# An LSTM recommender on one Trainium2 core: the head's bias sum moved to GpSimd, the sum over the days of the week to VectorE, and the opening of VectorE reordered

## What is computed

```python
rp = concat([region_tbl[region_idx], poi_tbl[poi_idx]])
nv = concat([rp @ W_rp + b_rp, coords @ W_co + b_co])
conv = elu(conv1d(nv, conv_w) + conv_b)                   # 8 steps of 32
emb = tanh(concat([car_tbl[car_idx], week_tbl[week_idx], time_tbl[time_idx]]))
x = concat([conv, emb for every step])
h = lstm_layer(x, Wih0, Whh0, bih0, bhh0)
h = lstm_layer(h, Wih1, Whh1, bih1, bhh1)
return ((h[:, -1] @ W1 + b1) @ W2 + b2) @ W3 + b3
```

## Time and profile before

| what | value |
|---|---|
| median of three runs | 1087.03 us |
| the profiled execution: time, and its span | 1081.45 us, 1079.6 us |
| TensorE busy | 1061.9 us, 98% |
| VectorE busy | 741.5 us, 69% |
| ScalarE busy | 516.4 us, 48% |
| GpSimd busy | 328.7 us, 30% |
| mean granted TensorE clock | 0.996 of full speed |
| chain that ended last | TensorE 88%, VectorE 6% |

### The profile page before, as it was taken

The page is one execution under the profiler, slowest core; times in us unless marked ns, Lnnn a source line. Parts: engine busy times, 40 slices in busy tenths (PEclk is TensorE's granted clock), DMA queues, the critical chain, the costliest instruction groups (busy, mean ns, idle before and its releaser), DMA issues.

```text
span 1079.6 us, 14388 instructions
## 1 busy us (share of the span) xinstructions
PE 1061.9 (98%) x4905; PEld 508.5 (47%) x4905; DVE 741.5 (69%) x1155; ACT 516.4 (48%) x757; POOL 328.7 (30%) x353
## 2 busy tenths in 40 slices
PE   8899999999999999999999999999999999999998
PEld 7544444444445444444445444444444444444445
DVE  6688866765767766666867865567676775666554
ACT  3665344454555444434554544345554544444433
POOL 7660255625410065533440045552450000000000
PEclk9899999999999999999999999999999999999999
DMA  9410100000101100000101010000010110000001
GB/s 265 84 18 1 31 2 3 2 1 2 31 1 40 31 4 3 2 2 2 16 18 40 1 34 2 2 2 1 2 31 1 40 30 0 2 0 1 1 1 39
DMA packets 32082, 21.26 MB, mean 20 GB/s; under 512 B 19629, under 2 KB 25865, under 8 KB 32019
## 3 DMA queue, kind: packets, MB, share of 16 engines
q1 hardware_dynamic: 21223, 19.25, 6.2%
q0 software_dynamic: 9984, 1.12, 2.6%
q10 hardware_dynamic: 812, 0.07, 0.1%
HBM read 9.92 MB, written 4.19 MB: 13 GB/s over the span
## 4 chain that ended last, share of the span: by engine, by line
PE 88%; DVE 6%; issue 2%; ACT 2%; SPq 1%; DMA 1%; DVEq 0%; ACTq 0%
PE acc L1509 49%; PE acc L1500 27%; PE acc L1494 4%; PE aux L1731 2%; SPq L495 1%; PE aux L1422 1%; PE acc L1562 1%; PE acc L1571 1%; ACT gates L835 1%; DVE h_full L1188 1%; DVE gates L1141 1%; DVE h_part L1189 1%; ACT tanh_c L840 1%; PE aux L1461 1%; DMA w_nat<-in_L_rec_Wih 1%
## 5 line engine op out<-in xcount | busy, mean ns | idle before, releaser
L1509 PE MATMUL acc<-h_part,wh 128*128 128x512 f16 (+1 forms) x2640 | 644.2, 380 | 0.0
L1509 PEld LDWEIGHTS acc<-h_part,wh 128*128 128x128 f16 x2640 | 240.3, 98 | 314.2 <-issue 54.6
L1500 PE MATMUL acc<-h_part,wh 128*128 128x512 f16 (+1 forms) x1440 | 346.8, 379 | 0.0
L835 ACT ACTIVATE gates<-acc,gate_bias,unscale 128x512 f32<-128x512 f32 x246 | 189.8, 778 | 303.2 <-PE acc L1509 283.6
L835 ACT ACTIVATE gates<-gates,gate_bias,unscale 128x512 f32<-128x512 f32 x242 | 188.6, 810 | 141.6 <-DVE gates L1141 141.0
L1500 PEld LDWEIGHTS acc<-h_part,wh 128*128 128x128 f16 x1440 | 139.9, 98 | 171.4 <-issue 4.8
L652 POOL DMA_INDIRECT feat<-in_L_rec_region_tbl,region_idx x160 | 162.1, 1013 | 165.0 <-PE acc L1509 132.8
L1141 DVE TENSOR_TENSOR gates<-acc,emb_gates 128x512 f32<-128x512 f32 x242 | 160.2, 685 | 42.5 <-PE acc L1509 33.4
L652 POOL DMA_INDIRECT feat<-in_L_rec_poi_tbl,poi_idx x120 | 121.4, 1012 | 109.6 <-PE acc L1509 97.3
L1494 PE MATMUL acc<-x_in,wx 96*128 96x512 f32 (+1 forms) x242 | 134.8, 563 | 3.7 <-DVE gates L1141 2.5
L1188 DVE TENSOR_TENSOR h_full<-gates,tanh_c 128x512 f32<-128x512 f32 x120 | 82.7, 689 | 75.3 <-ACT tanh_c L840 75.3
(11 more groups left out here) (182 smaller groups left out, 418.6 us busy)
## 6 DMA issues: line engine op xcount, KB each, us to landing
out<-y SPq DMA_DIRECT2D x16, 256.0 KB, 2.1
x_in<-conv_hi SPq DMA_DIRECT2D x56, 64.0 KB, 2.0
feat<-in_L_rec_region_tbl,region_idx POOLq DMA_INDIRECT x160, 2.3
w<-in_L_rec_W SPq DMA_DIRECT2D x4, 512.0 KB, 6.4
w_nat<-in_L_rec_Whh SPq DMA_DIRECT2D x2, 1024.0 KB, 8.6
w<-in_L_rec_W SPq DMA_DIRECT2D x1, 2048.0 KB, 11.9
feat<-in_L_rec_poi_tbl,poi_idx POOLq DMA_INDIRECT x120, 2.3
x_in<-conv_lo SPq DMA_DIRECT2D x28, 64.0 KB, 2.0
```

The lines of the kernel that those rows point to most:

```text
L835: nc.scalar.activation(gates[layer][:, j, g, :], source, ACT.Tanh if g == GATE_G else ACT.Sigmoid, bias=gate_bias[:, layer, m:m + 1], scal ...
L1500: mm = nc.tensor.matmul(bank, wh[:, 1, a, c, rows], h_part[0][:, s.write_slot, b, c, :], start=(c == 0 and a == b == HI), stop=(s.first an ...
L1509: mm = nc.tensor.matmul(bank, wh[:, own_w, a, c, rows], h_part[layer][:, s.read_slot, b, c, :], start=False, stop=(c == HK - 1 and a == LO))
```

## The change

Three things are moved.

1. VectorE's opening: the third row maximum goes from in front of `put_band` to behind `put_conv_bias`, and `row_scales(1)` goes behind `put_wx_lo`.
2. The sum over the days of the week: GpSimd keeps the product, and its copy and six adds become one `tensor_reduce` on VectorE, behind `add_biases`.
3. The head's constant: VectorE's eight instructions go. GpSimd, behind its last gather of the first batch, multiplies the eight slices of `w3` in place by their column of `b12` and adds them up in seven adds. TensorE's product with the ones stands in front of `cell(fifth)` and no longer behind it, and so does VectorE's add of b3.

```diff
--- before.py
+++ after.py
@@ -381,6 +381,7 @@
         w12_acc, w12_put = sem("w12_acc"), sem("w12_put")
         head_acc, head_hi_put, head_low_put = sem("head_acc"), sem("head_hi_put"), sem("head_low_put")
         b12_ready = sem("b12_ready")
+        head_sum_scaled = sem("head_sum_scaled")
         one_ready, head_sum_step, head_bias_acc, head_bias_put = (sem("one_ready"), sem("head_sum_step"),
                                                                   sem("head_bias_acc"), sem("head_bias_put"))
         coords_first_put = sem("coords_first_put")
@@ -618,12 +619,6 @@
                 nc.gpsimd.tensor_tensor(week_part[:, :, :, :], week_hot[:, :, :].unsqueeze(2).to_broadcast(rows),
                                         week_tbl[:, :, :].rearrange("p w d -> p d w").unsqueeze(1).to_broadcast(rows),
                                         ALU.mult).then_inc(week_step, 1)
-                pool.wait_ge(week_step, 2)
-                nc.gpsimd.tensor_copy(week_rows[:, :, :], week_part[:, :, :, 0]).then_inc(week_step, 1)
-                for day in range(1, WEEK):
-                    pool.wait_ge(week_step, day + 2)
-                    nc.gpsimd.tensor_tensor(week_rows[:, :, :], week_rows[:, :, :], week_part[:, :, :, day], ALU.add
-                                            ).then_inc(week_step if day + 1 < WEEK else week_put, 1)
 
             def poi_parts():
 
@@ -637,6 +632,21 @@
                         nc.gpsimd.tensor_tensor(poi_rest[:, k, :], rest[:, :] if k == 0 else poi_rest[:, k - 1, :],
                                                 poi_part[:, k, :], ALU.subtract).then_inc(poi_part_step, 1)
                         pool.wait_ge(poi_part_step, k + 1)
+
+            def sum_head_bias():
+
+                pool.wait_ge(head_acc, 2)
+                pool.wait_ge(b12_ready, 1)
+                for k in range(K2):
+                    nc.gpsimd.tensor_scalar(w3[:, k, :], w3[:, k, :], b12[:, k:k + 1], None, ALU.mult
+                                            ).then_inc(head_sum_scaled, 1)
+                pool.wait_ge(head_sum_scaled, 2)
+                nc.gpsimd.tensor_tensor(head_sum[:, :], w3[:, 0, :], w3[:, 1, :], ALU.add).then_inc(head_sum_step, 1)
+                for k in range(2, K2):
+                    pool.wait_ge(head_sum_scaled, k + 1)
+                    pool.wait_ge(head_sum_step, k - 1)
+                    nc.gpsimd.tensor_tensor(head_sum[:, :], head_sum[:, :], w3[:, k, :], ALU.add
+                                            ).then_inc(head_sum_step, 1)
 
             for n in range(NB):
                 tiles = None
@@ -703,6 +713,7 @@
                         landed = rows_in[0 if t < WIN else 1]
                         gather_steps(t, t + 1, False, landed)
                         pool.wait_ge(landed, (t - (PAIR_WIN if t < WIN else WIN) + 1) * GR * DMA)
+                    sum_head_bias()
                 else:
 
                     for c in range(CH):
@@ -967,6 +978,11 @@
                                         .to_broadcast([P, NB * GR, WEEK]),
                                         week_number[:, :].unsqueeze(1).to_broadcast([P, NB * GR, WEEK]),
                                         ALU.is_equal).then_inc(week_step, 1)
+            def sum_week():
+                dve.wait_ge(week_step, 2)
+                nc.vector.tensor_reduce(week_rows[:, :, :], week_part[:, :, :, :], AX.X, ALU.add
+                                        ).then_inc(week_put, 1)
+
             def row_maxima(i):
                 dve.wait_ge(w_in[i], DMA)
                 nc.vector.tensor_reduce(row_max[:, i, :], w_nat[i][:, :, :], AX.X, ALU.max,
@@ -1039,17 +1055,6 @@
                 dve.wait_ge(w12_put, K2)
                 dve.wait_ge(b2_put, 1)
                 nc.vector.tensor_tensor(b12[:, :], w12_t[:, :, H], b2_col[:, :], ALU.add).then_inc(b12_ready, 1)
-
-            def sum_head_bias():
-
-                dve.wait_ge(w3_in, DMA)
-                dve.wait_ge(b12_ready, 1)
-                nc.vector.tensor_scalar(head_sum[:, :], w3[:, 0, :], b12[:, 0:1], None, ALU.mult
-                                        ).then_inc(head_sum_step, 1)
-                for k in range(1, K2):
-                    dve.wait_ge(head_sum_step, k)
-                    nc.vector.scalar_tensor_tensor(head_sum[:, :], w3[:, k, :], b12[:, k:k + 1], head_sum[:, :],
-                                                   ALU.mult, ALU.add).then_inc(head_sum_step, 1)
 
             def put_head_lo(a):
                 dve.wait_ge(head_hi_put, a + 1)
@@ -1267,13 +1272,14 @@
             poi_one_hot(3, POI_PIECES)
             row_maxima(1)
             put_poi()
-            row_maxima(2)
             put_band()
             put_conv_bias()
+            row_maxima(2)
+            put_wx_lo()
             row_scales(1)
-            put_wx_lo()
             put_wh_lo(0)
             add_biases()
+            sum_week()
             elu(0, slice(0, HALF), (0, slice(0, HALF)), ())
             put_wh_lo(1)
             split_emb(0)
@@ -1297,14 +1303,13 @@
             indices(1, "region", REG, later, (later_idx_in, 2 * DMA))
             cell(third)
             cell(fourth)
-            sum_head_bias()
             dve.wait_ge(idx_ready, 2)
             indices(2, "poi", POI, later, (later_idx_in, 2 * DMA))
             elu(chunk_of(0, 1), slice(0, NCOL), (1, slice(0, NCOL)), [])
-            cell(fifth)
             dve.wait_ge(head_bias_acc, 1)
             dve.wait_ge(b3_in, DMA)
             nc.vector.tensor_tensor(b_head[:, :], aux[:, 0, :], b3_row[:, :], ALU.add).then_inc(head_bias_put, 1)
+            cell(fifth)
 
             for stage in stages(dve, NB, STEPS):
                 kind = stage[0]
@@ -1426,7 +1431,7 @@
 
             def sum_head_bias():
                 pe.wait_ge(one_ready, 1)
-                pe.wait_ge(head_sum_step, K2)
+                pe.wait_ge(head_sum_step, K2 - 1)
                 nc.tensor.matmul(aux[:, 0, :], one_col[:, 0:1].to_broadcast([P, P]), head_sum[:, :], start=True,
                                  stop=True).then_inc(head_bias_acc, 1)
 
```

## The result

| | before | after |
|---|---|---|
| median of six runs each, alternated | 1090.37 us (1086.82 to 1091.85) | 1099.26 us (1098.05 to 1099.39) |
| profiled execution, its span | 1081.45, 1079.6 us | 1098.76, 1096.9 us |
| GpSimd busy | 328.7 us | 350.2 us |

The change is **slower: ratio 1.0088, interval 1.0071 to 1.0104**, 8.9 us. The forecast was 0.9 us on a median of 1087.03, in a range that ended at 1093.2.

A forecast was written before the change was run, and what follows sets the result against it. TensorE, 98% busy, was taken to bound the kernel: the opening gains 4.0 us, VectorE's lag 2.1, the wait on GpSimd costs 6.9, so 0.9 us slower on 1087.03, 1087.9 us; range 1082.4 to 1093.2.

The forecast's parts named there:

- the gathers 2.6 us earlier: Opening: with the week's copy and adds off GpSimd, the next gather starts at 23.8 us, not 26.47, 2.65 us earlier.
- a wait in front of the ones' product: Before the fifth cell: TensorE waits 4 to 7 us for GpSimd's sum; 6.9 us was booked.
- two-input products on VectorE: Beside GpSimd's sum: VectorE's products with both inputs in SBUF take 1 to 2 us in place of 0.68.
- The adds, with their turns: GpSimd's head sum: seven adds at 1.50 us plus 0.06 between; turns with VectorE add 4.9 us over the whole sum.
- It costs nothing while that gap stays: Week's reduction on VectorE: its 0.4 us fits into VectorE's 0.90 us wait ahead of `elu`, and its readers come later.
- All later gathers are paced by GpSimd itself and by landings: First batch's later gathers on GpSimd: they also move 2.65 us earlier, so the engine comes free at 81.4 us.
- rival 4: Opening: rows land no earlier or GpSimd's pace isn't its own; GpSimd starts at 84.0 us, time 1090.5 us; 6%.
- The products: GpSimd's head sum: eight products of 128x512 with a column, 0.65 us each plus 0.06 between.
- rival 3: GpSimd's head sum: a product with a column costs an add's 1.56 us, not 0.71; time 1094.7 us; 12%.
- The sum: GpSimd's head sum before the fifth cell: 16.6 us alone plus 4.9 of turns with VectorE, from 81.4 to 102.9 us.
- VectorE's lag: Behind the fifth cell: 6.0 us of head bias work leaves VectorE, so TensorE's waits for it vanish, 2.1 us gained.
- The opening: First part of the kernel: earlier gathers and less idle time at the lower clock put TensorE 4.0 us earlier.

The follow-up runs named there:

- e9: Changed kernel with the week's sum left on GpSimd, VectorE's reduction gone: 1094.46 us, ratio 1.0054 to the kernel before; the changed kernel beside it took 1100.84 us.
- e2: Changed kernel with the ones' product and VectorE's add of b3 back behind the fifth cell, on the first chip: 1079.42 us, ratio 0.9988 to the kernel before.
- e3: Changed kernel with the head sum wholly back on VectorE and the ones' product behind the fifth cell, first chip: 1079.34 us, ratio 0.9988 to the kernel before.
- e6: Third chip: kernel before 1091.67 us, changed kernel 1099.88, changed with ones' product behind the fifth cell 1092.78, changed with head sum back on VectorE 1094.06.
- e4: Kernel before with only the week's reduction moved to VectorE, behind the biases, on the first chip: 1078.36 us, ratio 0.9981 to the kernel before.
- e8: Fourth chip: changed kernel 1099.62 us; kernel before with only the week's reduction on VectorE 1095.60; changed kernel with that reduction placed earlier 1109.29.
- e7: Second chip: week's reduction earlier on VectorE, in the changed kernel 1105.02 us, in the kernel before 1099.39; kernel before with 23 added GpSimd passes 1115.29.
- e1: Kernel before, unchanged, run again on the first chip: 1080.47 us, ratio 0.9997 to its other runs there.

## Why the prediction was wrong

Right were: the gathers 2.6 us earlier; a wait in front of the ones' product of 4 to 7 us (5.1 to 6.7 in all six profiles of the change); no gap behind it; two-input products on VectorE at 1 to 1.6 us beside the sum, evictions from PSUM unchanged at 1.87 for three. The adds, with their turns, were booked at 1.56 each plus a share of 4.9 us; they measured 1.28 once and 1.61 six times, turns taken in.

**The step that failed** is "It costs nothing while that gap stays ... Its readers, GpSimd's copy and SP's first stores of x, come later", and with it "All later gathers are paced by GpSimd itself and by landings". That was true of the one trace and is true on the first chip (36.30 against 38.60). But the reduction ties GpSimd's later gathers to VectorE's queue, while in the kernel before GpSimd waited for nothing of VectorE's there. On chips with slow issue VectorE is late: with the reduction in its program it stands 15.6 to 17.5 us at the points of interest, for nothing that the profile names. GpSimd now stands for 13.7 us, ends at 118.4 and not at 102.9, and TensorE, which comes at 113.4 where it came at 100.07, still waits for it. This was rival 4's condition ("GpSimd's pace is not its own"), priced at a start of 84.0 and given 6%; the start was 92.87. With the reduction off VectorE, 6.4 us of the 10.1 are gone (e9). How much of them needs VectorE's stand is not shown. An estimate from e9's rows: without the stand VectorE is past the biases at 46.0, a reduction there would let GpSimd go on at some 46.7 and not 51.5, the sum would end near 114, and TensorE would wait 1 to 2 us. So the tie alone would cost little; the tie and the stand together cost most of the 6.4.

**Mis-sized terms.** The products were taken at 0.65 us, from copies; they measured 1.70 in e2 and 1.81 after, and 1.48 at the least. That is rival 3's mechanism, at 12%. The sum took 24.6 us (e2) and 25.3 to 25.9 (the six profiles of the change), not 21.5. On chips with slow issue that alone costs next to nothing: in e9 the sum ends at 111.9 and TensorE comes at 112.34. VectorE's lag, booked at 2.1 us, was worth 0.1 (e2 against e3) or 1.3 (e6). The opening, booked at 4.0, gave 1.3 with the new order (e3) and 2.3 without it (e4), in part because the first rows were turned 0.9 us earlier and not 2.65. And the wait cost 1.5 us more than its length, for the clock behind it.

**What was under my eyes.** The profiled execution stood 5.6 us under the median of its three runs. I added the difference to the end as if it lay outside the places of the change. In e6 it lies in them (the ones' product at 132.42 and not 120.79): every slack read from that trace was that of an opening without the stall.

**What stays open.** The changed kernel never ran on the first chip. An estimate there, from e2: TensorE comes to the place at 98.35 (e2's convolution piece at 97.33 and its 1.02), the sum ends at 104.9, so 6.5 us of wait and 1.5 of clock on 1079.4, about 1087: slower than 1080.65 by some 0.6%, mostly for the dear products. Open too is the rest of 3.8 us in e9, and the 4.0 us that the reduction alone costs in e8. The opening's stall differs by program: the kernel with the reduction early takes 4.8 us (e7) and 9.7 us (e8) longer than the changed kernel, which differs in one line's place. That alone could hold both. Why the stall is there at all, and why VectorE's part of it comes with the reduction in its program, was not found. The Trainium skill (Runtime: NRT & Kernel Launch, "Instruction fetch mechanics") says that instructions stream in by blocks through a queue of the engine's own, at a cost that is mostly hidden; no run here shows whether that is what stalls.

No version beat the kernel before on both kinds of chip: the reduction alone gains 2.3 us on one (e4) and loses 4.0 on the other (e8).

## What to carry to other kernels

Before a small step moves to another engine, read what stands ahead of it in that engine's queue and whom that waits for: with 0.49 us of work on VectorE an engine that had run free was tied to one that was late, and without it the kernel was 6.4 us faster. A slack read from one trace is the slack of that execution; where the profiled time and the median differ by more than runs do, look for the difference before using any gap. And a relief counts only on the engine that the end waits for: 6 us taken off VectorE gave 0.1 to 1.3.

## What was not expected of the hardware

- Chips differ in the opening: with the same program and the same transfers TensorE gets 123 (e1) or 82 (e6) products through from 20 to 46 us. It is worth 11 us.
- The stall is not one engine's. VectorE stood up to 21.82 us (e8) with the product that it waits for long done, and TensorE 7.95 us for a copy by ScalarE (e9); which engine stands, and where, changes with the program.
- A GpSimd product of 128x512 takes 1.48 us at the least (e7) and 1.7 to 2.0 on average beside VectorE (e2, e9), where a copy of 384 elements takes 0.51.
- An add of GpSimd takes 1.26 to 1.28 us for 512 elements at the least. The Trainium skill (GPSIMD Engine Reference, "Side-by-side cycle accounting") gives 4497 ns for 2048 elements. A quarter of that, an estimate of 1.12 us, is nearer than my 1.50 from the small adds of the earlier trace rows.
- VectorE's products with both inputs in SBUF took 1.48 and 1.58 us beside the adds, and 0.68 alone. The Trainium skill (SBUF — State Buffer, "Who interferes with whom") says that the two exclude each other for the whole length of whichever came first; the trace agrees with a wait for an add under way: 0.8 and 0.9 us more, less than one add.
